# A spiking FFN on one core: the second batch's VectorE chain in PSUM, GpSimd adds beside it, and another order of stores

## The reference, cut to what matters

```python
rates  = relu(x) * 0.001                      # x: 2 x 2048 x 512
c      = cond[:, None, :] + cumsum(rates, axis=1)
spikes = (floor(c) - floor(c, one token earlier)) / 0.001
h      = relu(spikes @ w1 + b1)               # w1: 512 x 2048
out    = x + (h @ w2 + b2)                    # w2: 2048 x 512
```

## Time and profile before

| | us |
|---|---|
| median of three runs | 105.58 (104.89 to 106.0) |
| the profiled execution | 105.6 |
| its span, first to last instruction | 103.8 |
| PE, VectorE, GpSimd, ACT busy | 89.4, 64.9, 38.9, 36.3 |

### The profile page before, as it was taken

The page is one execution under the profiler, slowest core; times in us unless marked ns, Lnnn a source line. Parts: engine busy times, 40 slices in busy tenths (PEclk is TensorE's granted clock), DMA queues, the critical chain, the costliest instruction groups (busy, mean ns, idle before and its releaser), DMA issues.

```text
span 103.8 us, 1076 instructions
## 1 busy us (share of the span) xinstructions
PE 89.4 (86%) x325; PEld 45.4 (44%) x325; DVE 64.9 (63%) x148; ACT 36.3 (35%) x66; POOL 38.9 (37%) x43
## 2 busy tenths in 40 slices
PE   5999999999999999999989989999999999920000
PEld 5934444444644444554233326447666666500000
DVE  3448999969499999575848577999998000020000
ACT  2887515405182551459950000006622222200000
POOL 6220000000058700008700303599960578257850
PEclk9999999999999999999999999999999999998555
DMA  2999999999999999940000181899999999998871
GB/s 74 284 366 404 423 418 412 410 404 409 412 409 409 394 395 391 407 172 3 10 3 0 22 331 57 227 404 423 410 429 426 417 417 389 260 183 116 104 111 48
DMA packets 8203, 29.55 MB, mean 285 GB/s; under 512 B 1639, under 2 KB 1767, under 8 KB 6914
## 3 DMA queue, kind: packets, MB, share of 16 engines
q1 hardware_dynamic: 6192, 25.43, 62.3%
q0 software_dynamic: 1856, 4.00, 17.1%
q10 hardware_dynamic: 146, 0.01, 0.1%
HBM read 19.48 MB, written 10.75 MB: 291 GB/s over the span
## 4 chain that ended last, share of the span: by engine, by line
PE 46%; POOL 15%; DVE 14%; issue 12%; ACT 7%; POOLq 3%; DVEq 0%
PE ps_table L862 38%; POOL out L369 9%; DVE x_sb L724 6%; POOL x_sb L376 5%; PE ps_small L993 4%; ACT w_sb L444 3%; ACT w_sb L443 2%; POOLq L55 2%; PE ps_turn L899 2%; DVE place_hot L673 1%; PE ps_idle L888 1%; POOLq L277 1%; POOL out L401 1%; DVE under L599 1%; ACT block_sum L453 1%
## 5 line engine op out<-in xcount | busy, mean ns | idle before, releaser
L862 PE MATMUL ps_table<-w_sb 128*128 128x512 f32 x128 | 58.9, 607 | 0.0
L862 PEld LDWEIGHTS ps_table<-w_sb 128*128 128x128 f32 x128 | 23.7, 194 | 24.5 <-issue 23.2
L358 POOL DMA_INDIRECT rates<-in_x_turned,sixteen_at x8 | 9.8, 1224 | 36.0 <-DVE sixteen_at L603 34.2
L443 ACT ACTIVATE w_sb<-w_sb,b_col 128x512 f32<-128x512 f32 (+2 forms) x19 | 12.2, 643 | 16.5 <-DMA w_sb<-in_w_pairs 16.4
L589 DVE SCALAR_TENSOR_TENSOR total_two<-x_sb,total_two 128x1024 f32<-128x1024 f32 x14 | 17.1, 1224 | 1.2 <-DMA x_sb<-in_x 0.8
L967 PE MATMUL ps_table<-w_sb 128*128 128x512 f32 x32 | 16.4, 598 | 0.1
L369 POOL DMA_INDIRECT out<-w_sb,to_single x8 | 12.4, 1552 | 9.7 <-issue 6.5
L724 DVE TENSOR_TENSOR x_sb<-x_sb,ps_idle 128x2048 f32<-128x2048 f32 x6 | 13.3, 2280 | 0.0
L444 ACT ACTIVATE w_sb<-w_sb,minus_relu_b 128x512 f32<-128x512 f32 (+2 forms) x19 | 12.3, 649 | 0.6
L376 POOL TENSOR_TENSOR x_sb<-x_sb,idle_row 128x512 f32<-128x512 f32 x8 | 9.9, 1269 | 0.0
L547 DVE SCALAR_TENSOR_TENSOR idle_part<-w_sb,relu_b,idle_part 128x512 f32<-128x512 f32 x9 | 6.9, 763 | 1.6 <-DMA w_sb<-in_w_pairs 1.3
(11 more groups left out here) (135 smaller groups left out, 61.8 us busy)
## 6 DMA issues: line engine op xcount, KB each, us to landing
x_sb<-in_x SPq DMA_DIRECT2D x16, 512.0 KB, 14.8
out<-x_sb SPq DMA_DIRECT2D x8, 1024.0 KB, 7.2
w_sb<-in_w_pairs SPq DMA_DIRECT2D x15, 512.0 KB, 15.8
w_sb<-in_w_pairs SPq DMA_DIRECT2D x2, 256.0 KB, 2.9
b_row<-in_b SPq DMA_DIRECT2D x1, 256.0 KB, 14.8
rates<-in_x_turned,sixteen_at POOLq DMA_INDIRECT x8, 4.3
out<-w_sb,to_single POOLq DMA_INDIRECT x8, 6.3
w_sb<-in_w,w_at POOLq DMA_INDIRECT x2, 6.3
```

Of the source, the lines that this page charges most:

```text
L358: pool.indirect_dma_start(out=rates[:, col, :], out_offset=None, in_=x_sixteen, in_offset=bass.IndirectOffsetOnAxis(ap=sixteen_at[:, col:c ...
L443: chain(act.activation(weights, weights, ACT.Relu, bias=b1_col[:, m:m + 1], scale=PER_DT))
L862: last = pe.matmul(ps_table[c][:, :], table_hidden[:, m, c * P:(c + 1) * P], w2_sb[:, m, :], start=(m == 0), stop=(m == FC - 1))
```

## The change

Four things change together.

**VectorE's chain of batch 1 keeps its scratch in PSUM.** `climb_home[1]`, `rate_home[1]` and the others are pieces of the bank `ps_small`. Of two inputs of a VectorE operation in this chain at most one then lies in SBUF. `find_tokens(1)` gets two operations more.

**GpSimd adds the idle row to twelve token columns of batch 0** (before: eight of batch 1), from the moment on which VectorE has set `places_ready` for batch 0. Two columns stand ahead of the first `w1` gather, two between the gathers, eight behind the second. Each add now waits for the one before it. The gather of `general_x` moves from ahead of GpSimd's adds to between the two batches' scatters.

**VectorE's lists stand behind its adds.** After `list_places(1)` come one quarter of batch 0, `copy_rows` (two columns from PSUM, which now release PE's general part), four quarters of batch 1, and only then `list_singles`, `list_general` and `count_crowd`.

**SP stores the quarters in another order**, and PE's `sum_checks` stands behind step 10 of the general part, not 5.

```diff
@@ sync: store order
-            for b, q in ((0, 0), (0, 1), (0, 2), (0, 3), (1, 3), (1, 0), (1, 2), (1, 1)):
+            for b, q in ((0, 0), (0, 3), (1, 0), (0, 1), (1, 1), (0, 2), (1, 2), (1, 3)):
                 store_idle(b, q)
@@ gpsimd
             def add_idle(b, begin, end):
                 for t in range(begin, end):
-                    last = pool.tensor_tensor(x_sb[b][:, t, :], x_sb[b][:, t, :], idle_row[:, :], ALU.add)
+                    chain(pool.tensor_tensor(x_sb[b][:, t, :], x_sb[b][:, t, :], idle_row[:, :], ALU.add))
                     if t % TQ == TQ - 1:
-                        last.then_inc(idle_added[b][t // TQ], 1)
+                        pool.sem_inc(idle_added[b][t // TQ], 1)
...
+            pool.wait_ge(idle_copied, 1)
+            pool.wait_ge(places_ready, 1)
+            add_idle(0, 0, 2)
             get_w1(0)
-            pool.wait_ge(idle_copied, 1)
+            add_idle(0, 2, 4)
             get_w1(1)
-            pool.wait_ge(general_listed, 1)
-            pool.indirect_dma_start(out=general_x[:, :], out_offset=None, in_=x_rows,
-                                    in_offset=bass.IndirectOffsetOnAxis(ap=from_general[:, :], axis=0)
-                                    ).then_inc(general_got, 16)
-            add_idle(1, 12, 16)
-            add_idle(1, 8, 12)
+            add_idle(0, 4, 12)
             pool.wait_ge(singles_listed, 1)
             for b in range(B):
+                if b == 1:
+                    pool.wait_ge(general_listed, 1)
+                    pool.indirect_dma_start(out=general_x[:, :], out_offset=None, in_=x_rows,
+                                            in_offset=bass.IndirectOffsetOnAxis(ap=from_general[:, :], axis=0)
+                                            ).then_inc(general_got, 16)
                 pool.wait_ge(idle_stored[b], 16 * XQ)
@@ vector: find_tokens, the other steps of the chain are changed alike
-                chain(dve.tensor_tensor(climb[:, mine, :], climb[:, mine, :], over(sum_at[:, mine], BLK), ALU.add))
+                chain(dve.tensor_tensor(climb_home[b], climb_home[b], over(sum_at[:, mine], BLK), ALU.add))
...
+                else:
+                    chain(dve.tensor_tensor(under_home[b], climb_home[b][:, :, 0:BLK - 1], over(theta[:, 0, mine], BLK - 1),
+                                            ALU.is_lt))
+                    chain(dve.tensor_scalar(token_hot[:, mine, 0:1], under_home[b][:, :, 0:1], -1.0, 1.0, ALU.mult, ALU.add))
+                    chain(dve.tensor_tensor(token_hot[:, mine, 1:BLK], under_home[b], token_under[:, mine, 2:BLK + 1],
+                                            ALU.subtract))
@@ vector: order
             list_places(1)
+            add_idle(0, 12, 16)
+            copy_rows()
+            for q in range(XQ):
+                add_idle(1, q * TQ, (q + 1) * TQ)
             list_singles()
+            list_general()
             count_crowd()
-            list_general()
-            add_idle(0, 0, 4)
-            add_idle(0, 4, 8)
-            add_idle(0, 8, 12)
-            add_idle(0, 12, 16)
-            add_idle(1, 0, 4)
-            add_idle(1, 4, 8)
             judge()
@@ tensor
-            pe.wait_ge(general_listed, 1)
+            pe.wait_ge(rows_copied, 1)
...
-                if m == 5:
+                if m == 10:
                     sum_checks()
```

More of the change, by code:

```diff
@@ L79, in spike_ffn @@
         token_hot = sb("token_hot", [P, NE, BLK], BF16)
-        many = [sb(f"many{b}", [P, BLK]) for b in range(B)]
+        many = sb("many", [P, BLK])
         many_run = [sb(f"many_run{b}", [P, BLK], BF16) for b in range(B)]
@@ L128, in spike_ffn @@
         met = sb("met", [P, NE])
-        is_member = sb("is_member", [P, NE])
-        place = sb("place", [P, NE])
+        is_member = sb("is_member", [P, DC])
+        place = sb("place", [P, DC])
         row_at = sb("row_at", [P, NE])
@@ L183, in spike_ffn @@
         ps_hidden = [ps_turn, ps_small]
+        climb_home = [climb[:, :, :], ps_small[:, 64:128].rearrange("p (e t) -> p e t", e=DC)]
+        rate_home = [rates[:, 0:DC, :], ps_small[:, 0:64].rearrange("p (e t) -> p e t", e=DC)]
+        under_home = [token_under[:, 0:DC, 1:BLK],
+                      ps_small[:, 128:128 + DC * (BLK - 1)].rearrange("p (e t) -> p e t", e=DC)]
+        many_home = [many[:, :], ps_small[:, 192:192 + BLK]]
+        slot_home = [slot_part[:, :, :], ps_small[:, 208:208 + DC * BLK].rearrange("p (e t) -> p e t", e=DC)]
+        member_home = [is_member[:, :], ps_small[:, 272:272 + DC]]
+        place_home = [place[:, :], ps_small[:, 276:276 + DC]]
         ps_out = ps_table[0]
@@ L637, in find_general @@
                 dve.wait_ge(tokens_counted, b + 1)
-                chain(dve.tensor_scalar(many[b][:, :], ps_counts[b], 1.5, None, ALU.is_gt))
-                chain(dve.tensor_tensor_scan(many_run[b][:, :], ones[:, 0:BLK], many[b][:, :], 0.0, ALU.mult, ALU.add))
+                chain(dve.tensor_scalar(many_home[b], ps_counts[b], 1.5, None, ALU.is_gt))
+                chain(dve.tensor_tensor_scan(many_run[b][:, :], ones[:, 0:BLK], many_home[b], 0.0, ALU.mult, ALU.add))
                 chain(dve.tensor_copy(grid[b][:, BLK:2 * BLK], ps_counts[b]))
@@ L645, in number_general @@
                 chain(dve.scalar_tensor_tensor(out=grid[b][:, 0:BLK], in0=many_run[b][:, :], scalar=ps_before[b],
-                                               in1=many[b][:, :], op0=ALU.add, op1=ALU.mult))
+                                               in1=many_home[b], op0=ALU.add, op1=ALU.mult))
                 dve.sem_inc(general_numbered, 1)
@@ L659, in count_members @@
                 mine = own(b)
-                chain(dve.tensor_scalar(is_member[:, mine], facts_high[:, mine, 1:2].rearrange("p e o -> p (e o)"), 0.5, None,
+                chain(dve.tensor_scalar(member_home[b], facts_high[:, mine, 1:2].rearrange("p e o -> p (e o)"), 0.5, None,
                                         ALU.is_gt))
-                chain(dve.tensor_tensor_scan(member_run[b][:, :], ones[:, 0:DC], is_member[:, mine], 0.0, ALU.mult, ALU.add))
+                chain(dve.tensor_tensor_scan(member_run[b][:, :], ones[:, 0:DC], member_home[b], 0.0, ALU.mult, ALU.add))
                 dve.sem_inc(members_counted, 1)
@@ L670, in place_members @@
                 dve.wait_ge(members_before, b + 1)
-                chain(dve.scalar_tensor_tensor(out=place[:, mine], in0=member_run[b][:, :], scalar=ps_members[b],
-                                               in1=is_member[:, mine], op0=ALU.add, op1=ALU.mult))
-                chain(dve.tensor_tensor(place_hot[b][:, :, :], over(place[:, mine], P), along(slot_name, DC), ALU.is_equal))
+                chain(dve.scalar_tensor_tensor(out=place_home[b], in0=member_run[b][:, :], scalar=ps_members[b],
+                                               in1=member_home[b], op0=ALU.add, op1=ALU.mult))
+                chain(dve.tensor_tensor(place_hot[b][:, :, :], over(place_home[b], P), along(slot_name, DC), ALU.is_equal))
                 dve.sem_inc(places_ready, 1)
```

35 lines of the change are left out of this document (21 added, 14 removed).

## The result

The changed kernel took **108.56 us** (median of four runs, 108.22 to 108.86), the kernel before 105.79 beside it (104.89 to 106.06): a ratio of 1.0301, 95% interval 1.0244 to 1.0358. It is 3% slower, and outside the range. Some executions are disturbed and run longer: the ratios leave these out, the medians do not, and the profiles of chain_in_sbuf and batch0_first are of such executions. The profiled execution took 108.22 us with a span of 106.5, against 103.8.

The account below looks back on a forecast made before the run. Bound: the DMA engines carrying batch 0's four stores, then GpSimd's serial queue. First scatter 63.1 + 3.55 + 15.0 + 2.5 - 0.6 = 83.55, batch 1's at 92.25, then 11.76: span 104.0, with 1.8 outside 105.8 us; range 104.2 to 107.6.

Parts of the forecast that it names:

- The first store: SP's first store, behind four GpSimd adds and a w1 gather: issued at 63.1 instead of 68.11; 62.6 to 63.5.
- Batch 0's stores: DMA engines, first store to GpSimd's first scatter: six stores (15.0) and the second gather; scatter at 83.55, bounds 82.1 to 84.95.
- The term of the second gather: Second w1 gather falling among the stores in the DMA engines: 2.5 us at the stores' rate, or 2.8.
- my 3.55: Taken from the kernel before: first store's way, what was left of the gathers, and GpSimd's own start, 3.55 us.
- Between the scatters: GpSimd's queue: four scatters, 7.15, then general_x's gather, no store wait of 3.23; batch 1's first scatter at 92.25.
- The tail: From batch 1's first scatter to the end: nothing changed, 11.76 us.
- What I cost at nothing: GpSimd's eight later adds, VectorE's two more operations, its later lists, PE's delay and general_x's landing: all taken as covered.
- The first: DMA engines: stores no later than before, first scatter still at 81.66, time 103.9; chance 0.16.
- The second: GpSimd slowed beside VectorE's chain: adds of 1.8, first store 2.1 later, end at 107.9; chance 0.14.
- The third: general_x, gathered behind four scatters, lands after up to 10.3 us and sets the end, 108.9; chance 0.09.
- The fourth: VectorE's place_slot waits for GpSimd's add, twice up to 1.27, chain 2.5 late, 106.3; chance 0.05.
- my argument from that row: Against place_slot waiting for GpSimd: it takes 282 ns for 128 elements, a double-rate tensor_scalar 689 for 1024.

Follow-up runs that it names:

- chain_in_sbuf: The changed kernel with VectorE's chain of batch 1 back in SBUF, as before; 109.92 us, ratio 1.0416.
- batch0_first: The changed kernel with batch 0's four stores first, one added quarter swapped between VectorE and GpSimd, general_x gathered ahead of the scatters; 107.14 us, ratio 1.0087.
- hold_stores: The changed kernel, but all stores wait until the second w1 gather has landed; 108.56 us in one run.
- quarter_gather: The changed kernel, but the second w1 gather fetches a quarter of each row, leaving weights out; 104.42 us, ratio 0.9906.
- hold_adds: The changed kernel, but GpSimd's last eight adds wait until the second w1 gather has landed; 111.52 us in one run.
- first_hold: The changed kernel with batch 0's stores first, an added quarter swapped between VectorE and GpSimd, second store waiting for the second w1 gather; 106.56 us, ratio 1.015.
- hold_second: The changed kernel, but only the second store waits until the second w1 gather has landed; 108.80 us, ratio 1.0353.
- general_ahead: The changed kernel, but general_x is gathered ahead of batch 0's scatters; 107.86 us, ratio 1.026.
- first_between: The changed kernel with batch 0's stores first, an added quarter swapped between VectorE and GpSimd, general_x still between the scatters; 105.57 us, ratio 1.0034.

## Why the prediction was wrong, step by step

I forecast 105.8 us with a span of 104.0; the profile has 106.5. The 2.5 us between them are: first store -1.04, from there to the first scatter +2.82, from that scatter to batch 1's +0.06, and +0.65 behind.

- **The first store: forecast 63.1, issued at 62.06**, outside the bounds, on the early side. GpSimd began at 55.49, not 56.2, since VectorE's `place_hot` was itself 0.7 earlier in this execution; and the gap ahead of the gather was 0.29, not 0.78. The adds' pitch was right: two take 2.60 to 2.63. The error brought little, because the engines were full already, with the first gather: 429 GB/s over 62 to 65 us.
- **Batch 0's stores: the step that failed.** Six stores at 2.5 were right. The term of the second gather was not: 2.5, at most 2.8, against 4.6 (2.5 for its bytes and 2.1 in which the engines were held at a low rate). That the gather's time and the stores' add up was right: the stores do stand while it runs. Its size was wrong: I took its bytes, or the rate of two microseconds in the midst of a gather, and left out its slow start and what it loses beside queued stores. hold_stores shows 3.4 us of the engines for the gather alone, the changed kernel 3.9, and its gaps besides; quarter_gather shows that this gather is the cause, hold_adds that GpSimd's adds are not. Why a gather starts slowly, and why the stores do not move beside it, stays open. Of the other 0.7 of the 2.82, some 0.5, estimated from q0's bytes, is the first gather's remainder, which my 3.55 took from before: 0.42 MB in q0 from 62.06 on, against 0.20 from 68.11 on before (0.46, less the 0.26 of `general_x`). The upper bound 84.95 was summed from a first store at 63.6, where the text has 63.5; nothing hangs on it.
- **Between the scatters: right.** The wait of 3.23 is gone, `general_x` costs 1.3 in its place: 8.76 measured, 8.70 forecast.
- **The tail: 0.65 longer**, 12.41 against 11.76. Nearly all of it lies behind the last scatter's issue, whose landing took 3.8 us, before 3.3.
- **What I cost at nothing.** GpSimd's eight later adds ended at 75.12, ahead of need. The two operations more cost 0.6, within 0 to 1.0. PE waited 2.39 us for the gather, where I had allowed 3.0 at worst, and VectorE's row was still 3.4 us ahead of the scatter that needs it (98.1, needed at 101.5). `general_x` landed 3.9 us after its issue. All covers held.

PE's timeline of the changed kernel, the general part's first matmuls behind that wait:

```profile
72.66 0.68 PE L982 MATMUL ps_turn<-place_slot,w_sb 128*128 128x128 f32 x4 [2.39 <-DMA w_sb<-in_w,w_at]
```

**The rivals.** The first (stores no later, 103.9) is refuted: the bandwidth argued against it, rightly. The second (GpSimd slowed beside the chain) did not happen: its adds took 1271 ns on average, as in the earlier trace rows. The third (`general_x` sets the end) did not happen. The fourth, that `place_slot` waits for GpSimd's add, was real, though worth nothing here. VectorE's timeline of the changed kernel, where an add of GpSimd ended at 58.09:

```profile
57.60 0.58 DVE L701 TENSOR_SCALAR place_slot<-name_f,ps_turn 128x128 f32<-128x128 f32 x1
...
63.02 0.28 DVE L701 TENSOR_SCALAR place_slot<-name_f,ps_turn 128x128 f32<-128x128 f32 x1
```

The second stood beside an idle GpSimd and took the 0.28 of the earlier trace rows. So my argument from that row was wrong: the length of an operation that runs alone does not tell whether it waits for GpSimd. The Trainium skill ("SBUF — State Buffer", section Who interferes with whom) counts a `tensor_scalar` from SBUF to SBUF among those that can. These rows agree, as does the `tensor_scalar` of chain_in_sbuf (1.31 beside GpSimd's adds, 0.20 before).

What none of the four rivals had is what came true: that the second gather holds the engines for much longer than its bytes would, and the stores behind it as well.

## What to carry to other kernels

Where the DMA engines are the limit, an earlier first transfer is worth only what the engines have free at that moment; ask which other transfers it will now meet, and price these from the whole of one, its start too, and from a row in which they meet. The gather of rows among full-rate stores cost here 4.6 us for 2.5 us of bytes: try such a one ahead of the stores, or behind the last one that somebody waits for. And where the chain of waits names a path, move one thing on that path and one beside it before you believe it.

## What the runs showed of the hardware

- A gather of 1 MB in 128 rows landed 5.9 to 6.5 us after its issue when no store was beside it, 7.0 and 8.0 with one store flowing ahead of it (first_hold, hold_second), 8.9 to 10.0 with a second one queued (general_ahead the shortest, first_between the longest). Of the engines it took 3.4 us with no store, 3.2 and 3.6 with one ahead, 3.9 to 4.3 with a second one queued. Why is open: the runs show that it is not its bytes alone (2.5) and not GpSimd's adds (9.8 us to landing without them).
- While the second gather was under way (66 to 69 us of the changed kernel) the stores moved 0.02 MB, the gather 0.61.
- The engines' share tells little of the rate: 251 GB/s at 1.07 in first_between, 419 at 1.01, and 156 at 0.96 in the kernel before, at the start of its second gather, where no store was waiting:

```profile
65.00:66.00 1.00, 1.00 (x3) 0.38 (x2) 0.87 (x6) 0.00 (x0) 0.00 (x0) 1.00 0.96 156
```

- PE's wait for the late gather left a hole in its work at 70 to 72.7 us, and its granted clock over 71 to 80 us was 0.81 (in the windows above); over 74 to 76 us it was 0.50, the lower of the two levels, and from 77 on 1.00 again. In hold_stores, without the hole, it was 1.00 over 71 to 80. PE was not on the path here.
